# Setup of a graph network kernel: the chunk range of a half window by one comparison per direction, chunk rows by float32r products, and a 16-bit table of window positions

## The reference, cut to what matters

```python
agg = segment_sum(x[j], i, n)                     # layer 0: counts(dst, src) times x
attn = softmax over edges of a node, by dst       # layer 1: needs log of the counts
out0 = segment_sum(atten_e[:, None] * Mfeat[dst], src, n)   # layer 2: weighted sums
summed = segment_sum(x[src], dst, n)              # layer 3: counts again
```

## Time and profile before

| | before |
|---|---|
| runs shown | 1133.88, 1135.50, 1138.69 us (median 1135.50) |
| span of the profiled execution | 1133.4 us |
| TensorE busy | 1052.5 us (93%) |
| VectorE busy | 583.0 us (51%) |
| ScalarE busy | 445.4 us (39%) |
| setup, until the first product of the window loop | 0 to 57.2 us |
| building of the matrices, loop of 40 groups | 57.2 to some 217 us |
| the four layers | from there to the end |

### The profile page before, as it was taken

How to read it: one execution, slowest core, us unless ns; L and a number is a source line. 1 busy time by engine, 2 the same in 40 slices (tenths; PEclk the granted TensorE clock), 3 DMA queues, 4 the chain that set the end, 5 groups by cost and what they waited for, 6 DMA issues and landing times.

```text
span 1133.4 us, 16827 instructions
## 1 busy us (share of the span) xinstructions
PE 1052.5 (93%) x5904; PEld 689.2 (61%) x5904; DVE 583.0 (51%) x1743; ACT 445.4 (39%) x762; POOL 157.7 (14%) x182
## 2 busy tenths in 40 slices
PE   6988878899999999899999999999899998999998
PEld 3456656555444554677777777774456896555443
DVE  7888998610884011666665666655447337300133
ACT  6502565400645101565555656552436415410000
POOL 0000000000053000333333000005537012000000
PEclk9999998899999999999999999999999999999999
DMA  5003788850100000554544100026001051100010
GB/s 169 1 0 106 221 259 269 261 178 1 40 35 1 19 19 31 177 152 150 152 140 144 42 1 1 2 82 245 0 1 47 1 192 36 38 1 1 10 46 35
DMA packets 73097, 93.63 MB, mean 83 GB/s; under 512 B 7169, under 2 KB 63176, under 8 KB 73022
## 3 DMA queue, kind: packets, MB, share of 16 engines
q1 hardware_dynamic: 73022, 92.62, 26.1%
HBM read 58.00 MB, written 34.60 MB: 82 GB/s over the span
## 4 chain that ended last, share of the span: by engine, by line
PE 79%; DVE 10%; issue 5%; ACT 4%; DMA 1%; SPq 1%; DVEq 0%; ACTq 0%
PE PS L557 8%; PE PS L788 8%; PE PS L590 8%; PE PS L771 8%; PE PS L936 7%; PE PS L743 7%; PE PS L971 6%; PE PS L714 5%; PE PS L613 5%; PE PS L529 2%; DVE R L1241 2%; PE PS L700 2%; DVE HT L1106 2%; PE PS L891 2%; PE PS L918 2%
## 5 line engine op out<-in xcount | busy, mean ns | idle before, releaser
L557 PE MATMUL PS<-HT,R 125*128 125x313 bf16 x636 | 130.5, 351 | 27.0 <-DVE HT L1106 15.8
L1230 DVE CUSTOM_DVE_ANT_0 HT<-PS,CD 128x1250 f32<-128x1250 f32 (+1 forms) x80 | 116.4, 1455 | 67.4 <-issue 67.4
L557 PEld LDWEIGHTS PS<-HT,R 125*128 x636 | 98.0, 172 | 59.9 <-issue 45.4
L771 PE MATMUL PS<-K,HT 128*128 128x128 f32 (+2 forms) x800 | 112.5, 280 | 15.0 <-DVE R L1241 14.4
L1535 ACT COPY R<-PS 128x512 f32<-128x512 f32 (+1 forms) x120 | 64.8, 574 | 121.5 <-PE PS L771 119.5
L1555 ACT ACTIVATE HT<-HT,soft 128x1250 f32<-128x1250 f32 (+1 forms) x80 | 107.1, 1338 | 10.3 <-DVE soft L1233 3.3
L771 PEld LDWEIGHTS PS<-K,HT 128*128 128x128 f32 (+2 forms) x800 | 84.0, 140 | 43.2 <-DVE R L1241 23.6
L743 PE MATMUL PS<-R 64*128 64x512 f32 (+3 forms) x480 | 95.8, 531 | 3.1 <-DVE soft L1230 3.1
L788 PE MATMUL PS<-R 128*64 128x128 f32 (+2 forms) x1600 | 94.2, 273 | 0.0
L788 PEld LDWEIGHTS PS<-R 128*64 128x64 f32 (+1 forms) x1600 | 84.8, 137 | 6.4 <-issue 5.8
L590 PE MATMUL PS<-CD,H 128*128 128x512 f32 (+2 forms) x240 | 86.0, 520 | 2.4 <-ACT X L1445 2.4
(11 more groups left out here) (222 smaller groups left out, 1386.2 us busy)
## 6 DMA issues: line engine op xcount, KB each, us to landing
edge_parts<-X SPq DMA_DIRECT2D x160, 156.5 KB, 2.7
R<-edge_parts SPq DMA_DIRECT2D x60, 156.5 KB, 2.3
CD<-edge_sums SPq DMA_DIRECT2D x1, 6250.0 KB, 20.8
CD<-edge_parts SPq DMA_DIRECT2D x10, 469.5 KB, 3.8
BC<-edge_parts SPq DMA_DIRECT2D x30, 156.5 KB, 2.5
CD<-edge_parts SPq DMA_DIRECT2D x3, 1565.0 KB, 10.8
edge_sums<-R SPq DMA_DIRECT2D x20, 156.5 KB, 2.8
R<-edge_parts SPq DMA_DIRECT2D x18, 155.5 KB, 2.3
```

The lines of the kernel that those rows point to most:

```text
L557: return mm(bank(b0 + h, QUART), stat, hot, start=first, stop=True, skip_group_check=True)
L771: m = nc.tensor.transpose(PS[0:rows(j), o:o + n], Pb[u % 2][a][0:n, j * P:j * P + rows(j)], ident[0:n, 0:n])
L1230: ve.tensor_tensor_reduce(Pb[s][a][0:n], PS[0:n, a * N:(a + 1) * N], cd[0:n, t, :], 1.0, -3e38, ALU.add, ALU.max, soft[0:n, s, a:a + 1]).t ...
```

## The change

What it does:

- The comparison of a half window with a chunk took two conditions for each direction (the last dst of the chunk is not below the window, the first not above it) in two instructions. Now "up" takes only the first condition and "down" only the other, one instruction each, and three of the four no longer wait for each other. For sorted dst without empty half windows the results are the same.
- `diag` and a new copy of the ones, `ones_r`, are float32r, so the two products of `chunk_rows` are float32r. VectorE makes `ones_r` by a 128 x 128 copy at the head of its setup.
- `winI` is a table of uint16 in place of int32. To keep the positions above zero they carry SHIFT = 16384, which is taken off again in the index expressions.

```diff
+F32R = mybir.dt.float32r
+U16 = mybir.dt.uint16
+SHIFT = 16384
@@ buffers
+        cd_at = nc.sbuf_base
         CD = sb("CD", [P, T * N])
+        diag_r = nc.alloc_sbuf_tensor_at("diag_r", [P, 640], F32R, offset=cd_at)
+        ones_r = nc.alloc_sbuf_tensor_at("ones_r", [P, P], F32R, offset=cd_at + 4 * 5400)
-        winI = BC[0:1, 1200:1200 + NG * VALUES].bitcast(I32)
+        winI = BC[0:1, 1200:1200 + NG * VALUES].bitcast(U16)[:, 0:NG * VALUES]
-        diag = CD[0:80, 0:640].rearrange("p (a e) -> p a e", a=8)
+        diag = diag_r[0:80, :].rearrange("p (a e) -> p a e", a=8)
-        reach = CD[0:NW, 1400:2040].rearrange("p (q c) -> p q c", q=2)
@@ fixed_chunk, late_chunk
-            return bass.ds((d + m + (q - FIX)).with_bounds(min_val=q, max_val=NC - FIX - 1 + q), 1)
+            return bass.ds((d + m + (q - FIX - SHIFT)).with_bounds(min_val=q, max_val=NC - FIX - 1 + q), 1)
-            return bass.ds((d + m).with_bounds(min_val=FIX, max_val=NC - 1), 1)
+            return bass.ds((d + m + -SHIFT).with_bounds(min_val=FIX, max_val=NC - 1), 1)
@@ chunk_rows
-                mm(bank(4)[0:NW, 0:NC], K1[0:80, K_ONES:K_ONES + NW], diag[:, 0:4, :], start=True, stop=True)
-                mm(bank(2)[0:NW, 0:NC], K1[0:80, K_ONES:K_ONES + NW], diag[:, 4:8, :], start=True, stop=True).then_inc(sem("setup_ps"), 1)
+                mm(bank(4)[0:NW, 0:NC], ones_r[0:80, 0:NW], diag[:, 0:4, :], start=True, stop=True)
+                mm(bank(2)[0:NW, 0:NC], ones_r[0:80, 0:NW], diag[:, 4:8, :], start=True, stop=True).then_inc(sem("setup_ps"), 1)
@@ vector engine
             dve.wait_ge(sem("rows_io"), 2 * 16)
+            ve.tensor_copy(ones_r[:, :], K1[:, K_ONES:K_ONES + P])
             link(ve.tensor_copy(growF, growI))
@@
-                for q, k in ((0, K2_UP), (1, K2_DOWN)):
-                    link(ve.scalar_tensor_tensor(reach[:, q, :], last, K1[0:NW, K_TLO + h:K_TLO + h + 1], K2[:, k:k + NC],
-                                                 ALU.is_ge, ALU.mult))
-                    link(ve.scalar_tensor_tensor(span[:, q, h, :], first, K1[0:NW, K_THI + h:K_THI + h + 1],
-                                                 reach[:, q, :], ALU.is_le, ALU.mult))
+                ve.scalar_tensor_tensor(span[:, 0, h, :], first, K1[0:NW, K_THI + h:K_THI + h + 1],
+                                        K2[:, K2_UP:K2_UP + NC], ALU.is_le, ALU.mult)
+                i = ve.scalar_tensor_tensor(span[:, 1, h, :], last, K1[0:NW, K_TLO + h:K_TLO + h + 1],
+                                            K2[:, K2_DOWN:K2_DOWN + NC], ALU.is_ge, ALU.mult)
+            link(i)
@@
-                    link(ve.tensor_scalar(ends, ends, 1.0 - FIX, None, ALU.add))
+                    link(ve.tensor_scalar(ends, ends, 1.0 - FIX - SHIFT, None, ALU.add))
```

## The result

The changed kernel takes 1183.5 us (median of 6 runs, 1179.5 to 1184.6), the kernel before 1134.7 us on the same chip (6 runs): a ratio of 1.043, interval 1.041 to 1.046. That is 48.8 us slower and lies far outside the forecast range. The profiled execution of the changed kernel has a span of 1177.5 us, 44.1 more than before.

A forecast was written before the change was run, and what follows sets the result against it. TensorE, busy 93%, was taken to bound the kernel, with VectorE near the bound in the window loop. The span of 1133.4 plus 1.5 for the shift, other terms 0, plus 2.1 to the median run gave 1137.0 us; range 1131.5 to 1141.5.

The forecast's parts named there:

- The 16-bit table: Register loads of 20 values on TensorE and VectorE in the window loop: no change, as registers, not bytes, set the price.
- the upper end: Bound for slower table loads: nine loads at the longest, 2.73 us, in place of the median, 2.26, cost 4.2 us.
- a rival that made them shorter: Table loads: 16-bit loads take half the time, half of TensorE's gain exposed, -5 us, total 1132 us; chance 0.10.
- The comparisons: Setup: eight become four, 2.5 us leave VectorE, its wait for `ranges` grows from 0.95 to 3.4 us; gain 0.
- The copy of the ones: Head of VectorE's setup: one 220 ns copy, `chunk_rows` starts at 7.28 in place of 7.06; cost 0.
- The float32r products: Setup on TensorE: between 2.4 us as now and next to nothing; line 519 still waits for ScalarE until 9.64; 0.
- The shift: Late steps' index expressions: a fourth register operation, 14 ns on TensorE, at most 18 on VectorE; +1.5 us.
- The rival that put 10.1 us in line: Window loop: added register operation in line in each late step, two first-group iterations over 2.35 us; 1145.6 us, chance 0.06.
- The later rise of the clock: TensorE's first tiles in the setup: clock rises one tile later, at most +3.6 us, 1140.6 with the shift; chance 0.07.

The follow-up runs named there:

- int32_shift: The changed kernel with an int32 table, loop ends masked to 16 bits, SHIFT = 16384 kept: 1137.7 us, ratio 1.001 to the kernel before.
- int32_twice: int32_table with each of the ten register loads of each engine given twice: 1155.1 us, ratio 1.018 to the kernel before.
- int32_table: The changed kernel with the table int32 again, SHIFT = 0 and loop ends masked to 16 bits: 1137.2 us, ratio 1.001 to the kernel before.

## Why the prediction was wrong

**The 16-bit table** is the step that failed: "the same 20 registers take 1.39 to 2.73 us, so bytes are not what varies. I take no change", with 4.2 us as the upper end. Measured, it is +46 us by the time (1183.5 against the 1137.7 of `int32_shift`; 47 if each is taken against the kernel before on its own chip) and +51 us by TensorE's loads. The argument was that the number of registers sets the price and bytes do not. But the ten loads of the earlier trace rows have the same number of registers and the same number of bytes, so their spread from 1.39 to 2.73 us tells nothing of either. They were all of one kind, int32 on a multiple of 16 bytes, and could not tell registers from reads. By reads the numbers fit: the shortest aligned loads are 578 ns for 5 registers (2 reads), 845 for 12 words (3 reads), 1349 for 20 (5 reads, `int32_twice`), some 270 to 290 ns a read; the first load of 20 in the changed kernel takes 4906 ns, 245 for each register. How the chip reads was inferred from these times, not seen. The upper end was wrong in kind too: it came from the spread of the rows shown (2.73 against 2.26), and the spread of one kind of load bounds nothing about another. No row priced a single register.

The Trainium skill (Runtime: NRT & Kernel Launch, Instruction fetch mechanics) puts a register load at some 200 ns per register, even in bulk. It says so of what the runtime loads in its preamble, and the section names neither width nor place. The runs have two prices for the loads of `winI`: 245 ns per register off the aligned int32 case (4906 ns for 20), near the page's figure, and 77 ns within it (1547 ns for 20). By the page 20 registers would be 4 us, an estimate, 1.7 us above the median of 2.26, and nine such loads would add some 16 us: a wider upper end than 4.2 us, though still a third of what came.

**How the loads reach the time** was half right. The prediction saw that "TensorE's loads are long and VectorE waits right behind them", in a rival that made them shorter. It took half of a gain as exposed; `int32_twice` shows 17.9 us of time for 18.4 us of loads, nearly all of it. Longer loads stood only in the bound of 4.2 us and were no rival with a time and a chance.

**The comparisons**: priced 0, right. 2.7 us left VectorE (4.6 to 1.9 us), and the wait for `ranges` grew by 1.95; the comparisons began 0.3 us later, and TensorE gave `ranges` 0.45 us sooner (27.21 against 27.66), which makes up the rest and why 2.90 was measured where 3.4 was forecast. **The copy of the ones**: 227 ns against 220, but it ran from 3.58 us, 0.11 ahead of the first cast's old start, and hid the rest: `chunk_rows` started at 7.08, not at 7.28. **The float32r products**: between the bounds, 0.8 us in place of 2.4, and no time: line 524 started at 9.96 for ScalarE. The forecast had 9.64.

**The shift**: +9 ns in the late steps on TensorE (44 ns each in the first group's loop before, 53 after) and +12 on VectorE (55 to 67), below the 14 and 18 taken as ends. The 37 to 64 ns of the earlier trace rows mix late and fixed steps, and the 37 is not the first group's, whose first fixed steps take 46, so the 14 ns per operation was misread; `int32_shift` is 0.5 us above `int32_table`, inside both intervals. +1.5 us was somewhat too much and changes nothing. The rival that put 10.1 us in line falls: the two runs with and without it differ by 0.5 us, and two iterations of the first group take 2.21 us (line 1130 starts at 60.00 and at 62.21), not over 2.35.

**The later rise of the clock** did not come. In the same view as the earlier trace rows, which had 4.90 and 3.60 us, the first two tiles of line 534 are:

```profile
13.46 4.64 PE L534 MATMUL PS<-WA,CD 128*128 128x512 f32 x8
...
18.71 3.60 PE L534 MATMUL PS<-WA,CD 128*128 128x512 f32 x8
```

In both kernels the first two products of the first tile take 1.06 us each and the last ones 0.59; the third takes 1.04 us before and 0.79 after. So the rise came no later with 0.8 us of work in place of 2.4 in front. It is read from these durations; the column of the granted clock reads 1.00 over the whole stretch in both traces. By the rule of the Trainium skill (TensorE: Matmul & The Clock Gate, Part 1) that the warm-up is a matter of time and not of a number of products, less busy time in front could have meant a later rise; these two executions show no such effect.

Of the four parts (comparisons, float32r products with their copy, shift, table), then, three were priced rightly within what the runs can tell, and the sum without the table (1137.0) is near what `int32_shift` measured (1137.7). The failed one was 46 to 47 us of the 48.8; an upper end of 4.2 us for an operation that no row showed was the real mistake.

## What to carry to other kernels

Keep values that an engine reads into registers in 4-byte words, start each load on a multiple of 16 bytes, and fill it with whole fours; here a narrower table saved no time and cost 46 us, and forty loads of five values took 33 us against 20 for ten loads of 20. Where a sequencer loads registers in the middle of a loop of waits, as here, the load can be in line on whichever engine has the longer one: look at the queue rows of the profile, since the engine rows call it only "issue". And where a change alters the type or the place of an operand, the rows of before are about another instruction, and their spread bounds nothing about the new one: a bound then needs the price of its smallest piece times their number, or a small experiment.

## What the runs showed of the hardware that was not expected

- A load of 20 registers takes 1.35 to 1.61 us at the quickest for int32 on a multiple of 16 bytes, and 4.7 to 4.9 us for 16-bit values (packed, or each in a word of its own; signed or unsigned) or for int32 that is 4 bytes off. 8 bytes off is as slow (10 registers: 3.1 us, as with 16-bit values at that point of the loop, against 1.3).
- The same load is slower in the stretch with stores: 4.9 us at 51 us, up to 8.6 us later; int32 1.5 us, up to 2.7. TensorE's longest is 1.8 times its first in both kinds. That the stores cause this was not tested by itself.
- A fourth operation in a fused register instruction costs 9 ns on TensorE (44 to 53 in the late steps) and 12 ns on VectorE (55 to 67).
- TensorE's float32r product of 80 x 80 by 80 x 320 takes 0.47 to 0.55 us as a single record; as float32 it was two records and 1.2 us.
